# Cross-attention scores: the first row tile's matmuls in turn over four row groups and four PSUM banks

## What is computed

```python
x = _layernorm(x + _L0_attn_ref(x, ...))                 # delta rule + MLP
q = proj(query, Wq, bq)                                  # 16 heads of 16 features
k = proj(key, Wk, bk)
v = proj(value, Wv, bv)
scores = jnp.einsum('bhqd,bhkd->bhqk', q, k) / math.sqrt(D_K)
p_attn = jax.nn.softmax(scores, axis=-1)
x = jnp.einsum('bhqk,bhkd->bhqd', p_attn, v)
...
x = _layernorm(x + _L0_ffn_ref(x, ...))                  # experts
```

## Time and profile before

| | us |
|---|---|
| median of 3 runs | 1871.33 |
| lowest, highest | 1869.11, 1872.06 |
| span of the profiled execution | 1868.3 |
| TensorE busy | 1319.0 |
| VectorE busy | 1255.1 |
| POOL busy | 1008.7 |
| ScalarE busy | 834.4 |

### The profile page before, as it was taken

How to read it: one execution, slowest core, us unless ns; L and a number is a source line. 1 busy time by engine, 2 the same in 40 slices (tenths; PEclk the granted TensorE clock), 3 DMA queues, 4 the chain that set the end, 5 groups by cost and what they waited for, 6 DMA issues and landing times. The chain is left out here.

```text
span 1868.3 us, 32990 instructions
## 1 busy us (share of the span) xinstructions
PE 1319.0 (71%) x8936; PEld 1144.7 (61%) x8937; DVE 1255.1 (67%) x3313; ACT 834.4 (45%) x2767; POOL 1008.7 (54%) x1250
## 2 busy tenths in 40 slices
PE   6604558700036676766765899998489999999997
PEld 4403446500024455655654778877389999999997
DVE  4499999999988999999876144454434444443442
ACT  5522224501103666666866488887323322322332
POOL 3258998887669999998866425342111122122121
PEclk9857778955567887878867999998689999999999
DMA  4611113540031000100102212133130410411200
GB/s 117 204 40 35 47 41 112 175 125 0 17 125 38 23 28 23 33 27 27 28 28 79 62 35 59 50 124 115 45 102 21 147 55 20 154 48 45 77 17 7
DMA packets 108409, 119.22 MB, mean 64 GB/s; under 512 B 22769, under 2 KB 87720, under 8 KB 106280
## 3 DMA queue, kind: packets, MB, share of 16 engines
q1 hardware_dynamic: 70760, 90.98, 15.6%
q10 hardware_dynamic: 33136, 18.58, 3.4%
q0 software_dynamic: 4432, 8.73, 1.4%
HBM read 83.44 MB, written 35.74 MB: 64 GB/s over the span
## 5 line engine op out<-in xcount | busy, mean ns | idle before, releaser
L242 POOL TENSOR_TENSOR wt<-wt 128x1024 f32<-128x1024 f32 x128 | 301.3, 2354 | 47.1 <-DVE wt L187 32.2
L248 POOL TENSOR_TENSOR wt<-wt 128x512 f32<-128x512 f32 (+2 forms) x384 | 306.8, 799 | 30.1
L1902 PE MATMUL e_ph<-e_g,e_w 128*128 128x128 f32 x2496 | 285.2, 275 | 0.7 <-ACT e_g L1872 0.7
L1902 PEld LDWEIGHTS e_ph<-e_g,e_w 128*128 128x128 f32 x2496 | 281.9, 192 | 0.9 <-issue 0.9
L187 DVE SCALAR_TENSOR_TENSOR wt<-wt,scan 128x256 f32<-128x256 f32 x512 | 244.8, 478 | 1.8 <-POOL wt L242 1.8
L166 DVE TENSOR_REDUCE wt<-wt 128x16 f32<-128x272 f32 x512 | 222.2, 434 | 0.1
L177 DVE TENSOR_TENSOR scan<-wt,scan 128x256 f32<-128x256 f32 x512 | 217.8, 425 | 0.3
L155 DVE TENSOR_TENSOR wt<-wt,scan 128x256 f32<-128x256 f32 x512 | 213.0, 416 | 0.5 <-PEq L265 0.5
L1380 ACT ACTIVATE wt<-p_pX,p_mx 128x120 f32<-128x120 f32 x512 | 176.4, 387 | 71.7 <-DVE p_mx L1165 71.5
L1781 POOL TENSOR_TENSOR e_ve<-e_mv,eps 128x1 f32<-128x1 f32 x39 | 7.4, 189 | 330.9 <-DVE e_mv L1837 330.9
L1863 ACT ACTIVATE e_g<-e_ph,wt 128x128 f32<-128x128 f32 x156 | 48.7, 363 | 304.9 <-PE e_ph L1902 304.9
(11 more groups left out here) (226 smaller groups left out, 2814.5 us busy)
## 6 DMA issues: line engine op xcount, KB each, us to landing
wt<-in_L_ffn_W SPq DMA_DIRECT2D x24, 1024.0 KB, 5.2
qkv<-f_st ACTq DMA_DIRECT2D x48, 256.0 KB, 2.3
p_kE<-kE SPq DMA_DIRECT2D x16, 480.0 KB, 3.8
p_vP<-vP SPq DMA_DIRECT2D x16, 480.0 KB, 4.5
wt<-qkv SPq DMA_DIRECT2D x6, 1024.0 KB, 9.9
e_xt<-routed ACTq DMA_DIRECT2D x39, 130.0 KB, 2.1
f_xt<-in_x SPq DMA_DIRECT2D x16, 256.0 KB, 2.8
p_oT<-o SPq DMA_DIRECT2D x16, 256.0 KB, 2.9
```

What stands on the lines that cost most here:

```text
L242: nc.gpsimd.tensor_tensor(x, s["S"][:, h, z * Q:(z + 1) * Q], s["qn"][:, h, z * Q:(z + 1) * Q].rearrange("p t (o d) -> p t o d", o=1).to_b ...
L248: nc.gpsimd.tensor_tensor(x[:, :, :, 0:half], x[:, :, :, 0:half], x[:, :, :, half:2 * half], ALU.add).then_inc(s["o_fold"][h], 1)
L1902: ins = nc.tensor.matmul(ph2[:, c // 2, c % 2], w2[:, s, i, c * P:(c + 1) * P], g1[:, i], start=(i == 0), stop=(i == C1 - 1))
```

## The change

Score 0 now issues the matmuls of all four row groups, with the groups in turn inside g, into the four banks; score 1 is no longer called. Both signals of `score_done` are kept: one comes after the second group's last matmul, one after the fourth's. Ahead of it stands one wait, for all eight copies of item d, where there had been a wait for six before score 0 and one for eight before score 1. Scores 2 and 3, the second row tile, keep their groups, their places and their order.

```diff
                 if x >= 2:
                     pe.wait_ge(exp_done, c * HALVES + (x - 1))
+                groups = range(4) if x == 0 else range(x % 2 * 2, x % 2 * 2 + 2)
                 for g in range(G):
-
-                    for i in range(2):
-                        group = x % 2 * 2 + i
+                    for group in groups:
                         rows = slice(32 * group, 32 * group + 32)
-                        ins = nc.tensor.matmul(pX[:, x % 2, i, g * 2 * CTX:(g + 1) * 2 * CTX], qT[rows, g, q * P:(q + 1) * P],
+                        ins = nc.tensor.matmul(pX[:, group // 2, group % 2, g * 2 * CTX:(g + 1) * 2 * CTX], qT[rows, g, q * P:(q + 1) * P],
                                                kE[rows, q, g].rearrange("p a c -> p (a c)"), start=True, stop=True)
-                ins.then_inc(score_done, 1)
+                        if g == G - 1 and group % 2:
+                            ins.then_inc(score_done, 1)
...
                 if "c" in on:
                     if "d" in on:
-                        pe.wait_ge(PT_out, d * 8 + 6)
+                        pe.wait_ge(PT_out, d * 8 + 8)
                     score(c, 0)
-                    if "d" in on:
-                        pe.wait_ge(PT_out, d * 8 + 8)
-                    score(c, 1)
```

## The result

The changed kernel takes 1879.01 us (median of four runs, 1873.77 to 1881.25), the kernel before 1870.22 us beside it. The ratio is 1.0041 with a 95% interval of 1.0028 to 1.0053, that is 7.7 us (5.2 to 9.9) slower. The four runs of the changed kernel scatter over 7.5 us, the four of before beside them over 3.1 us (the 26 of before beside e1 to e4 over 10.0 us, 1865.75 to 1875.79). The profiled execution of the changed kernel is the fastest of its four, with a span of 1872.1 us; the other three took 1878.96 to 1881.25 us, and no trace shows what one of them was like.

What follows compares the result with a forecast made beforehand. Limits in turn: VectorE around 700 to 800 us, TensorE around 1100 to 1200, experts from 1300. Terms 2.54 + 0.90 + 2.70 + 0.90 + 0.2 = 7.2 us on the profiled span; as a median 1878.5 us, range 1874.0 to 1883.5.

Steps and rivals of the forecast that it cites:

- The wait goes first; the matmuls gain nothing on the path.: Score stage: all sixteen matmul records start 0.05 us after the eighth copy; the first call's 0.8 us lay under ScalarE's copies.
- The delay of the first maximum: VectorE's first maximum comes later by the distance between the two score calls' starts: 0.81 to 0.97 us, 0.90 in pair 11.
- Pairs 10, 11, 12: Hardware loop: ScalarE loads its table only after the maximum, so the delay reaches the third score call; 3 x 0.90 = 2.70 us.
- Pairs 9, 13, 14: Table loaded ahead; in pair 13, 1.37 us of cover for a delay of 0.90 us; cost 0.
- Pair 15: Last pair: no down product between, third call waits for the exponentials, route into the experts hangs on it; 0.90 us.
- The clock: Rival: longer TensorE pauses halve its clock once in each of six pairs; +10.2 us, 1888.7 us; chance 0.07.
- The first half: Pairs 0 to 7: delayed maxima of pairs 1, 5, 6 (2.54 us) and 7 (0.90 us) cost 3.4 us.
- this is not given back at the step's end: Pairs 1, 5, 6, likewise 7: VectorE's whole queue moves by the delay; 2.54 us, plus 0.90 for pair 7.
- The term for pair 1: VectorE waits for the scores there, then runs scan work back to back, so its queue moves by 0.92 us.
- Faster: Rival, pairs 9 to 14: both calls take 1.04 us together, not 1.82, saving 4.7 us; 1866.6 us; chance 0.05.
- Swallowed: Rival: the scan's slack absorbs the first half's cost, leaving pairs 10 to 12 and 15; 3.8 us, 1875.1 us; chance 0.13.
- Does not do what it says: Rival: four groups in turn run only two at a time, records take 1.82 us; +8.8 us more, 1887.3 us; chance 0.05.

Runs made afterwards that it cites:

- e1: Kernel before with its two score calls kept, the first call's wait for six copies made eight; 1.0044 of the kernel before, 8.2 us slower.
- e4: Changed kernel plus one small ScalarE exponential ahead of the wait for the first maximum, loading the table early; 1.0018 of the kernel before, 3.4 us slower.
- e3: The change in pairs 8 to 15 only, other pairs as in the kernel before; 1.0017 of the kernel before, 3.2 us slower.
- e11: The change in pairs 0 to 7 only, with the token number on ScalarE instead of VectorE; 1.0029 of the kernel before, 5.4 us slower.
- e9: Kernel before with the token number computed by ScalarE instead of VectorE; 1.0013 of the kernel before, 2.4 us slower.
- e2: The change in pairs 0 to 7 only, other pairs as in the kernel before; 1.0029 of the kernel before, 5.4 us slower.
- e10: Changed kernel with the token number computed by ScalarE instead of VectorE; 1.0044 of the kernel before, 8.2 us slower.
- e8: The change in pairs 0, 1, 5, 6 and 7 only, other pairs as in the kernel before; 1.0010 of the kernel before, 1.9 us slower.
- e6: The change in pairs 2 to 4 only, other pairs as in the kernel before; 0.9999 of the kernel before, -0.2 us.
- e5: Kernel before plus one small ScalarE exponential ahead of the wait for the first maximum; 0.9996 of the kernel before, -0.7 us.

## Why the prediction was right, point by point

**Sign and size.** 1878.5 us against 1879.01, and +7.2 us against 7.7 (5.2 to 9.9). The second half's share is right with its mechanism; that the first half's 3.4 us fits as well is in part luck, as shown below.

**"The wait goes first; the matmuls gain nothing on the path."** Right, and shown: e1 has the old matmuls and the same loss. The reading that decided it was that the second call started 0.05 us after the last copy, together with the undivided piece of sixteen in pair 8.

**The delay of the first maximum, 0.90 us.** Right where the steps are written out: in pair 7 the maximum had waited 1.34 us (at 984.35) and waits 2.25, the first of the rows below. In the loop steps it is 0.98 (2.31 from 1.33): their first score call starts 0.12 us after the copy that it waits for, where that of the written-out steps starts 0.05 us after it. I had taken 0.05 from the second call of pair 11. The term was small by 0.07 us, three times, and the down product of pair 11 starts 0.08 us later behind the last copy (1.14 from 1.06) and not 0.03. In pairs 5 and 6 the wait grew by 0.81 us, as forecast. In pair 1 it did not: the forecast had it longer by 0.9 us, and in this trace it went from 1.05 us to nothing. Three rows of the changed kernel: the maximum of pair 7, the third calls of pairs 13 and 15.

```profile
985.41 1.16 DVE L1165 TENSOR_REDUCE p_mx<-p_pX 128x8 f32<-128x960 f32 x1 [2.25 <-PE p_pX L1559]
...
1248.83 1.08 PE L1559 MATMUL p_pX<-p_kE,p_qT 32*128 32x240 f32 x8
...
1311.19 1.57 PE L1559 MATMUL p_pX<-p_kE,p_qT 32*128 32x240 f32 x6 [1.87 <-ACT wt L1380]
```

**Pairs 10, 11, 12, 2.70 us.** Right in place and cause: 34.88 from 33.88 twice, 34.73 from 33.79 once, 2.9 us in all, and e4 takes it back by loading the table early. **Pairs 9, 13, 14, nothing:** the third call of pair 13 starts 1248.83 without a wait, and the step from pair 13 to 14 is 31.71 us, before 31.69. **Pair 15, 0.90 us:** its third call's wait for the exponentials, 1.35 us in the earlier trace rows, is 1.87 us at 1311.19; the distance from pair 8 to 15 as a whole grows by 3.6 us (4.2 in e3), and the timed e3 gives 3.2. The clock stayed at 1.00, as said, from 1082 to 1287 us.

**The first half, 3.4 us.** The sum is near the measured 3.0 (e11 against e9) to 5.4 (e2), but the way to it does not hold, and the agreement is partly luck. The step "this is not given back at the step's end", for pairs 5, 6 and 7, does not hold in general. If each delay passed on, the distance from the maximum of pair 5 to that of pair 8 would grow by 0.81 + 0.90 = 1.7 us (pair 8 has no delay of its own, pair 5's is inside its own start). It grew by 0.1 in the changed kernel, shrank by 0.6, 0.5 and 0.2 in e1, e2 and e10, and grew by 2.7, 2.2 and 2.0 in e4, e8 and e11.

The term for pair 1, 0.92 us, was paid in e2, e4 and e8 and not in the traces of the changed kernel, e1, e10 and e11. And pairs 2 to 4 were counted at nothing because VectorE comes late by itself. They are nothing by their own scores (e6), but the token number waits longer for POOL in them, by 3.0 us in e2, e4 and e8, where VectorE had waited for the scores of pair 1 (and by 1.4 us in the changed kernel's trace, where it had not).

From the maximum of pair 0 to that of pair 8 it is 463.6 to 464.5 us with the code of before (before, e3, e5). With the change it is 461.4 us in e10, 464.2 in e1, 465.2 in its own trace, 466.8 in e11, 468.0 in e2 and 471.0 and 470.6 in e4 and e8. So single executions spread from about 3 us gained to 7 us lost, and the forecast 3.4 lies in their middle. Which path ends last differs from one execution to the next. What sets it is not settled; that the first half's timed cost (e2) is larger than that of its two parts (e6, e8) is open too, since the intervals are as wide as the gap.

**The rivals.** "Faster" decided itself nowhere: in pair 11 the last copy ends 0.88 us after TensorE has finished the transposes. "Swallowed" holds for pairs 5 to 7 in four of seven traces, yet the timed first half lost all the same (e2, 3.6 to 7.1 us), by the wait for POOL in e2's trace. The clock did not fall between 1082 and 1287 us, and e4, with the same pause, shows the loop steps at their old length. "Does not do what it says" was excluded by the piece of 1.09 us.

## What to carry to other kernels

Before packing matmuls over more row groups, look at what starts the second batch: here it was another engine's copy, and the first batch had been running under it at no cost. Merging two steps with different waits gives both the later one, and the price is read from the wait of the earlier step's reader, less what cover it has. Here the cover was a table load that lay ahead of the wait or behind it, so look at each form of the step: it was tight in the loop and slack written out.

## What the runs showed that I had not expected

A 128 x 2 VectorE instruction (L1193) took from 0.13 to 2.33 us, and whenever it took over 0.25 us it ended within 0.03 us of the POOL instruction beside it. With it the back-to-back steps of VectorE between pairs 1 and 4 vary from 58.3 to 60.4 us. Taking it away fixed them at 58.1 to 58.2 us but did not shorten the total. And two calls over different row groups run side by side by themselves: their eight matmuls, sent to the groups 0, 1, 0, 1, 2, 3, 2, 3 in this order, took 1.11 us in one piece (sixteen records), against 1.09 us in turn over four.
